# Second attention of a two-layer model: VectorE's small jobs moved between the two maxima of the next half slot

## The chip, the cores and the metric

The kernel runs on one core of a Trainium2 chip. Its engines work side by side, each through its own list of instructions in order: TensorE (PE, matmuls and transposes), VectorE (DVE), ScalarE (ACT), GpSimd (POOL) and SyncE (SP, which here only issues transfers). They wait for each other through semaphores. The metric is the device time of one execution in microseconds (us); the times shown are the median of three runs.

## The reference

Two layers over 8 sequences of 512 tokens with 128 features. Layer 0 is an attention with 16 heads of 64 and a relative position term, and a mixture of 8 experts, two for each token. Layer 1 is a second attention and a mixture of 8 experts with a capacity of 160 tokens. After each of the four comes the residual sum and a layer norm. The change touches only the second attention:

```python
mixed_q = hidden_states @ wq + bq
mixed_k = hidden_states @ wk + bk
mixed_v = hidden_states @ wv + bv
glo = jnp.mean(mixed_q, axis=1, keepdims=True)
c = jnp.tanh(mixed_q @ wfq + bfq + (glo @ wfg + bfg))
...
P = jax.nn.sigmoid(p) * key_len
Z = jax.nn.sigmoid(z) * key_len
G = -(j[None, None, None, :] - P[..., None]) ** 2 * 2.0 / Z[..., None] ** 2
...
scores = jnp.einsum('bhqd,bhkd->bhqk', q, k) / jnp.sqrt(jnp.float32(D))
scores = scores + G
probs = jax.nn.softmax(scores, axis=-1)
ctx = jnp.einsum('bhqk,bhkd->bhqd', probs, v)
```

It has 16 heads of 8. p and z are sums of c over a head with weights.

## The kernel before

The second attention (`gauss_attention_phase`) goes through the 8 batches one after the other: a first one, six middle ones in a hardware loop, a last one, and a tail that drains what is left. A batch has 16 slots, four for each of four groups of heads. A slot has two halves, "middle" and "end"; below, 9M and 9E are the two halves of slot 9.

In each half TensorE computes, in this order: a score tile of 128 queries by 512 keys for one head into bank `a_s0`, a transposed score tile for a later stage into `a_st`, a second score tile for another head into bank `a_s1`, and a second transposed tile (`scores`, L1768 and L1772). Then come eight value matmuls of an earlier unit into `a_pv` (L1804). VectorE reads each score tile and takes the negated row maximum (`maxima`, L1932, into `a_nm`). A score tile of the next half may be written only when the maximum over the same bank is done (`max_done`). ScalarE takes the exponential of the two transposed tiles (L1890). The maxima of a group are transposed (nm0 to nm3, L1829), stored in half precision and put by a transfer into a row of the query operand, so that the transposed scores have them subtracted.

Between these runs a series of small jobs that all use one shared PSUM bank, `a_misc`. Their places are written out by hand in two tables, `MIDDLE` and `END` (L1272 to L1274), one job at most in each half. TensorE fills the bank, then ScalarE, VectorE or both read it; TensorE may fill it for the next job when all earlier readers are done (`misc_out`). The jobs are:

- for the batch ahead: XT (transposed tokens, L1387; ScalarE writes the high part, VectorE subtracts it for the low part, L1484), Q, K and F (three matmuls each, L1396 to L1398, read by ScalarE), GB (a gate bias, VectorE, L1494), PZ (L1420, ScalarE's exponential, then VectorE's three steps for the centres, L1501 to L1503), CF (transposed coefficients, L1428, ScalarE), V (L1407 to L1409, VectorE's copy, L1490)
- for the batch at hand: ctx0 and nm0 to nm3 (ScalarE reads these)
- for the batch behind: ctx1 to ctx3 (a transpose, L1815, then VectorE's reciprocal and product, L1938 and L1940), CT (L1821, ScalarE high, VectorE low), OUT (output projection; VectorE's sum, statistics and their aggregation, L1947, L109, L114), RX (transposed normalised rows, L1836, ScalarE high, VectorE low), RL (router logits, L1843 to L1845, VectorE)
- RC and RD, the routing counts, in the last batch and the tail only

`norm` is the end of the second attention's layer norm: VectorE normalises four tiles (L122), GpSimd makes two copies of the result, SyncE stores rows. It waits for an inverse deviation that GpSimd computes after OUT.

`schedule` (L1671 on) is one function that every engine runs with its own table of steps, so all engines go through the same order. `shared_use` finds the batch for a job and calls the engine's step.

Of the kernel before, what the change touches and what calls it, by code (L numbers as in the profile page):

```python
# [82 lines left out]
class Steps:  # L83
# [12 lines left out]
    def step(self, ins):  # L96
        self.done(ins)
        self.wait()
# [1140 lines left out]
def routing_memory(nc, ctx, m):  # L1239
# [24 lines left out]
G = 4  # L1264
# [3 lines left out]
NM_LOADS = 2 * 16  # L1268
PARTS = 7 * 16
ZERO_PARTS = 8  # L1270
PREP = ["XT", "Q", "K", "GB", "F", "PZ", "CF", "V"]
MIDDLE = {4: "nm0", 8: "nm1", 9: "CT", 10: "OUT", 12: "nm2", 13: "RX", 15: "RD"}  # L1272
END = {0: "ctx1", 1: "XT", 2: "Q", 3: "RC", 4: "ctx2", 5: "K", 6: "GB", 7: "F", 8: "ctx3", 9: "PZ", 11: "CF", 12: "ctx0",
       13: "V", 14: "RL", 15: "nm3"}  # L1274
SLOTS = 4 * G
EXPS_AT = {("last", 1): 0, ("tail", 0): 1, ("tail", 15): 2}
CHOSEN_AT = {("last", 2): 0, ("tail", 1): 1, ("tail", 15): 2}
# [6 lines left out]
def part_of(name):  # L1284
    return name if name in ("RC", "RD") else "ahead" if name in PREP else "behind" if name in BEHIND else "own"

def uses(kind):
    order = [t[at] for at in range(SLOTS) for t in (MIDDLE, END) if at in t]
    return [u for u in order if part_of(u) in PARTS_OF[kind]]

def use(kind, b, name):

    if kind == "prep0":
        return PREP.index(name)
    base = len(PREP)
    if kind != "first":
        base = base + len(uses("first")) + len(uses("middle")) * ((b if kind == "middle" else B - 1) - 1)
    if kind == "tail":
        base = base + len(uses("last"))
    return base + uses(kind).index(name)  # L1300
# [313 lines left out]
def gauss_attention_phase(nc, io, out, m):  # L1614
# [8 lines left out]
    with ExitStack() as ctx:  # L1623
# [13 lines left out]
        ct_h, ct_l = (sb(n, [P, S], F16) for n in ("a_ct_h", "a_ct_l"))  # L1637
# [3 lines left out]
        xr_h, xr_l = (sb(n, [P, S], F16) for n in ("a_xr_h", "a_xr_l"))  # L1641
        res = sb("a_res", [P, QC, D], F32)
        scale = [sb(f"a_scale{k}", [P, QC], F32) for k in range(4)]
        r = m.r
# [16 lines left out]
        ct_hi, pvs_done, ctx_steps, xres_done = names("ct_hi", "pvs_done", "ctx_steps", "xres_done")  # L1661
        s_mm, max_done, exp_done = ([sem(f"a_{n}{k}") for k in range(2)] for n in ("s_mm", "max_done", "exp_done"))
        st_mm = g_.st_mm
        nm_in = [sem(f"a_nm_in{g}") for g in range(G)]
# [3 lines left out]
        def schedule(eng, do):  # L1668

            def step(name, *args):
                if name in do:
                    do[name](*args)

            def shared_use(name, kind, b):
                part = part_of(name)
                if part in PARTS_OF[kind]:
                    batch = {"ahead": b + 1, "behind": b - 1}.get(part, b)
                    if name[-1] in "0123":  # L1680
                        step(name[:-1], kind, b, batch, int(name[-1]))
                    else:
                        step(name, kind, b, batch)

            def batch(kind, b):
                behind, own = kind != "first", kind != "tail"
                for at in range(SLOTS):
                    g, s = divmod(at, G)
                    step("slot", kind, b, at)
                    head = (b, g, s) if own else None  # L1690
                    unit = ((b, (at - 6) // G, (at - 6) % G, kind == "first" and at == 6) if at >= 6 and own
                            else (b - 1, (at + 10) // G, (at + 10) % G, False) if at < 6 and behind else None)
                    for half, table in ((0, MIDDLE), (1, END)):
                        step("scores", half, head, unit)
                        if kind == "tail" and at == 6:
                            step("value", b - 1, G - 1, QC - 1, half)
                        if half and s == 2 and (at < 8 and behind or at >= 8 and own):
                            step("group_end", *((b - 1, g + 2) if at < 8 else (b, g - 2)))
                        if at in table:
                            shared_use(table[at], kind, b)  # L1700
                    if at == 11 and behind:
                        step("norm", b - 1)

            step("setup")
            batch("first", 0)
            with eng.Fori(1, B - 1) as b:
                batch("middle", b)
            batch("last", B - 1)
            batch("tail", B)
# [197 lines left out]
        def _(dve):  # L1907
# [9 lines left out]

            used, low, turns = prep.dve(dve)

            def maxima(half, head, unit):  # L1920
                if not head:
                    return
                b, g, s = head
                n = 16 * b + 4 * g + s
                if s == 0 and half == 0:

                    dve.wait_ge(nm_in[(g + 2) % G], NM_LOADS * (b + 1) if g >= 2 else NM_LOADS * b)
                c = 2 * (s % 2) + half
                for j in range(2):
                    hh = 2 * (s // 2) + j  # L1930
                    dve.wait_ge(s_mm[j], 2 * n + half + 1)
                    nc.vector.tensor_reduce(nm[g % 2][:, c, hh:hh + 1], s_ps[j][:, :], AX.X, ALU.max,  # L1932
                                            negate=True).then_inc(max_done[j], 1)

            def context(kind, b, cb, g):
                used(kind, b, f"ctx{g}")
# [48 lines left out]
            def place(name):  # L1985
                def run(kind, b, _):
                    h = INSTALMENT[kind, name]
                    (c0, n), c1, hs, k = ROUTED[h], sum(ROUTED[h]), slice(ROUTED[h][0], sum(ROUTED[h])), prefix_in[0]
                    used(kind, b, name)
                    nc.vector.tensor_copy(r.counts[h][:, :], misc[:, 0:2 * n * E1]).then_inc(misc_out, 1)  # L1990
                    dve.wait_ge(misc_out, use(kind, b, name) + 1)
                    running = r.counts[h][:, 0:n * E1].rearrange("p (c e) -> p c e", e=E1)
                    totals = r.counts[h][:, n * E1:].rearrange("p (c e) -> p c e", e=E1)
                    if h == 0:
                        routing.done(nc.vector.memset(r.prefix[k][:, 0:1, :], 0.0))
                    else:
                        before = r.counts[h - 1][:, (2 * ROUTED[h - 1][1] - 1) * E1:].unsqueeze(1)
                        routing.done(nc.vector.tensor_tensor(r.prefix[k][:, c0:c0 + 1, :], r.prefix[k][:, c0 - 1:c0, :], before, ALU.add))
                    routing.step(nc.vector.tensor_copy(r.prefix[k][:, c0 + 1:c1, :], totals[:, 0:n - 1, :]))
                    d = 1  # L2000
                    while d < n:
                        old, new = r.prefix[k], r.prefix[1 - k]
                        routing.done(nc.vector.tensor_copy(new[:, c0:c0 + d, :], old[:, c0:c0 + d, :]))
                        routing.step(nc.vector.tensor_tensor(new[:, c0 + d:c1, :], old[:, c0 + d:c1, :], old[:, c0:c1 - d, :], ALU.add))
                        k, d = 1 - k, 2 * d
                    prefix_in[0] = k
                    routing.step(nc.vector.tensor_tensor(r.held[:, hs, :], running, r.prefix[k][:, hs, :], ALU.add))
                    routing.step(nc.vector.tensor_tensor(r.onehot_pos[:, hs, :], r.held[:, hs, :], r.onehot[:, hs, :], ALU.mult))
                    routing.step(nc.vector.tensor_reduce(r.pos[:, hs], r.onehot_pos[:, hs, :], AX.X, ALU.add))

                    routing.done(nc.vector.scalar_tensor_tensor(r.slot[:, hs], r.best[:, hs], float(CAP), r.pos[:, hs], ALU.mult, ALU.add))
                    routing.done(nc.vector.tensor_scalar(r.over[:, hs], r.pos[:, hs], float(CAP), None, ALU.is_gt))
                    routing.step(nc.vector.tensor_scalar(r.away[:, hs], r.best[:, hs], float(NT), OUT_OF_RANGE, ALU.mult, ALU.add))
                    routing.step(nc.vector.tensor_tensor(r.over[:, hs], r.over[:, hs], r.away[:, hs], ALU.mult))
                    routing.step(nc.vector.scalar_tensor_tensor(r.slot[:, hs], r.slot[:, hs], -1.0, r.over[:, hs], ALU.add, ALU.add))
                    nc.vector.tensor_copy(r.to_slot[:, hs], r.slot[:, hs]).then_inc(r.slots_done, 1)
                return run

            def slot(kind, b, at):
# [6 lines left out]
                if (kind, at) in CHOSEN_AT:  # L2026
                    choose(CHOSEN_AT[kind, at])

            schedule(dve, {"slot": slot, "RX": low("RX", xr_h, xr_l, r.rx_hi), "RL": logits, "RC": place("RC"), "RD": place("RD"), **turns, "scores": maxima, "ctx": context, "CT": low("CT", ct_h, ct_l, ct_hi), "OUT": output, "norm": norm})

        @block.gpsimd
        def _(pool):
# [343 lines left out]
```

## Time and profile before

| | |
|---|---|
| median of three runs | 1611.47 us (1609.98 to 1611.98) |
| profiled execution | 1612.34 us |
| its span, first to last instruction | 1610.6 us |
| busy: PE | 1448.2 us, 90% |
| busy: DVE | 1116.6 us, 69% |
| busy: ACT | 956.0 us, 59% |
| busy: POOL | 755.3 us, 47% |
| second attention, first to last score | 1046.2 to 1519.0 us |
| mean granted TensorE clock | 0.962 |

The profile is one execution. Each engine's busy time is the sum of its instructions; a PE that is busy is not one at its peak, since two matmuls on different rows of the array run at once and both are counted. The rows that matter here are single instructions in order of time, because the change moves work by less than a microsecond many times over. The granted clock is 1.00 where TensorE runs at its full 2.4 GHz and 0.5 where it runs at 1.2 GHz.

### The profile page before, as it was taken

The numbers are of one execution on the slowest core, as the hardware profiler recorded it, in microseconds if no ns is written. First come the engines' busy times: TensorE is split into PE (matmuls) and PEld (weight loads), VectorE is DVE, ScalarE is ACT, GpSimd is POOL, SyncE is SP. The second block draws the span as 40 slices with busy tenths as digits, with TensorE's granted clock in tenths as the row PEclk, the third lists the DMA queues.
The fourth block names the chain that finished last, engine by engine and source line by source line (L and its number), as shares of the span: only waits on it lengthen the run. The fifth ranks groups of instructions, "written<-read, shape, count | busy, mean of one in ns | idle before, by whom it ended". The sixth has DMA issues, their size and how long they took to land. (4 is left out here: it accounts for less than half of the span.)

```text
span 1610.6 us, 37407 instructions
## 1 busy us (share of the span) xinstructions
PE 1448.2 (90%) x12185; PEld 808.4 (50%) x12185; DVE 1116.6 (69%) x2581; ACT 956.0 (59%) x2056; POOL 755.3 (47%) x944
## 2 busy tenths in 40 slices
PE   5999999999999999999978998878888888887837
PEld 3666666666666666666655666522333332332225
DVE  5567666666757657666677777778888888888732
ACT  2555555555555555555556887737667677675721
POOL 4656656655665665665564444511222231232633
PEclk9999999999999999999989999959999999999968
DMA  6101000000100000000000000150111111111000
GB/s 193 26 21 28 22 20 23 23 20 20 26 20 20 26 20 20 22 25 20 20 17 2 0 0 1 37 156 24 51 33 36 43 33 49 36 36 34 18 24 17
DMA packets 71099, 50.82 MB, mean 32 GB/s; under 512 B 30875, under 2 KB 59408, under 8 KB 70896
## 3 DMA queue, kind: packets, MB, share of 16 engines
q1 hardware_dynamic: 67936, 45.70, 10.3%
q10 hardware_dynamic: 1760, 3.02, 0.6%
q0 software_dynamic: 1344, 1.33, 0.3%
q8 instruction: 35, 0.57, 0.2%
q14 instruction: 24, 0.20, 0.1%
HBM read 38.18 MB, written 13.28 MB: 32 GB/s over the span
## 5 line engine op out<-in xcount | busy, mean ns | idle before, releaser
L608 ACT ACTIVATE prob<-score_ps,nmax 128x512 f32<-128x512 f32 (+3 forms) x512 | 266.8, 528 | 181.7 <-DVE nmax L669 181.7
L669 DVE TENSOR_REDUCE nmax<-score_ps 128x1 f32<-128x512 f32 (+3 forms) x512 | 225.0, 481 | 200.2 <-PE score_ps L488 195.4
L1932 DVE TENSOR_REDUCE a_nm<-a_s 128x1 f16<-128x512 f32 x512 | 324.0, 685 | 46.1 <-PE a_s L1768 43.6
L1890 ACT ACTIVATE a_pt<-a_st 128x1024 f32<-128x1024 f32 x256 | 261.7, 1024 | 122.1 <-PE a_st L1772 121.3
L1768 PE MATMUL a_s<-a_kop,a_qop 64*128 64x512 f16 x512 | 185.0, 405 | 62.6 <-DVE a_nm L1932 54.6
L786 POOL TENSOR_SCALAR_AFFINE_SELECT k_h<-k 64x512 f16<-64x512 f32 x130 | 79.1, 609 | 266.7 <-ACT k L635 256.4
L500 PE MATMUL pt_ps<-ident,prob 128*128 128x128 f32 x1280 | 186.2, 276 | 2.4 <-ACT pt L617 1.4
L617 ACT ACTIVATE pt<-pt_ps 128x512 f32<-128x512 f32 (+1 forms) x192 | 102.9, 536 | 139.4 <-PE pt_ps L500 139.4
L1772 PE MATMUL a_st<-a_qop,a_kop 64*128 64x512 f16 x512 | 175.1, 395 | 0.0
L1804 PE MATMUL a_pv<-a_pt,a_vaug 128*32 128x256 f32 x2048 | 167.4, 399 | 8.0 <-ACT a_pvs L1895 6.1
L789 POOL TENSOR_TENSOR k_l<-k,k_h 64x512 f16<-64x512 f32 x130 | 152.6, 1174 | 10.8
L500 PEld LDWEIGHTS pt_ps<-ident,prob 128*128 128x128 f32 x1280 | 140.6, 141 | 33.7 <-issue 11.6
L789 POOL TENSOR_TENSOR q_l<-q,q_h 128x512 f16<-128x512 f32 x130 | 151.1, 1162 | 10.8
L485 PE MATMUL score_ps<-k_h,q_h 128*128 128x512 f16 (+3 forms) x512 | 153.6, 300 | 0.6 <-POOL q_l L789 0.6
L486 PE MATMUL score_ps<-k_l,q_h 128*128 128x512 f16 (+3 forms) x512 | 153.6, 300 | 0.0
L487 PE MATMUL score_ps<-k_h,q_l 128*128 128x512 f16 (+3 forms) x512 | 153.4, 300 | 0.0
L512 PE MATMUL pv_ps<-pt,v 128*64 128x512 f32 (+3 forms) x1024 | 151.9, 439 | 0.0
L684 DVE COPY pt<-pt_ps 128x512 f32<-128x512 f32 (+1 forms) x192 | 114.7, 597 | 49.6 <-PE pt_ps L500 47.2
L1768 PEld LDWEIGHTS a_s<-a_kop,a_qop 64*128 64x128 f16 x512 | 41.7, 94 | 184.6 <-DVE a_nm L1932 144.9
L512 PEld LDWEIGHTS pv_ps<-pt,v 128*64 128x64 f32 x1024 | 67.9, 136 | 115.8 <-issue 106.2
L689 DVE SCALAR_TENSOR_TENSOR q<-proj_ps,q_bias,q_mult 128x512 f32<-128x512 f32 x130 | 97.3, 748 | 28.2 <-PE proj_ps L456 27.9
L1210 POOL TENSOR_TENSOR hid_l<-hid,hid_h 128x512 f16<-128x512 f32 x65 | 75.3, 1162 | 78.9 <-ACT hid_h L1115 78.7
(376 smaller groups left out, 3038.6 us busy)
## 6 DMA issues: line engine op xcount, KB each, us to landing
r_bc<-r_parts SPq DMA_DIRECT2D x128, 128.0 KB, 2.8
a_qop<-q_parts SPq DMA_DIRECT2D x64, 64.0 KB, 1.9
a_kop<-k_parts SPq DMA_DIRECT2D x64, 64.0 KB, 1.9
x_tok<-in_L_attn_input_dram SPq DMA_DIRECT2D x4, 512.0 KB, 12.4
r_parts<-rsum SPq DMA_DIRECT2D x128, 2.0 KB, 2.1
q_parts<-a_q_h SPq DMA_DIRECT2D x16, 128.0 KB, 2.3
k_parts<-a_k_h SPq DMA_DIRECT2D x16, 128.0 KB, 2.3
e_w<-in_L_ffn_w_dram SPq DMA_DIRECT2D x1, 2048.0 KB, 10.5
```

Source lines behind the costliest of these rows:

```text
L485: nc.tensor.matmul(o, q_h[h][:, qs], m.k_h[h][:, 0:w], start=True, stop=False)
L486: nc.tensor.matmul(o, q_h[h][:, qs], m.k_l[h][:, 0:w], start=False, stop=False)
L500: mm = nc.tensor.transpose(pt_ps[use % 2][:, col + (c - j) * P:col + (c - j + 1) * P], prob[h][:, P_OFF[c] + j * P:P_OFF[c] + (j + 1) * P] ...
L512: mm = nc.tensor.matmul(pv_ps[64 * h:64 * h + 64, j * P:S], v32[k][:, j, 64 * h:64 * h + 64], pt[h][k][:, J_OFF[j]:J_OFF[j] + S - j * P], ...
L608: ins = nc.scalar.activation(prob[h][:, P_OFF[c]:P_OFF[c] + w], score_ps[u][:, col:col + w], ACT.Exp, bias=nmax[h][:, c:c + 1], accum_out= ...
L669: ins = nc.vector.tensor_reduce(nmax[h][:, c:c + 1], score_ps[u][:, col:col + P * (c + 1)], AX.X, ALU.max, negate=True)
L789: return nc.gpsimd.tensor_tensor(lo, src, hi, ALU.subtract)
L1768: nc.tensor.matmul(s_ps[j][:, :], qop[tile_rows[j], t, g, c * P:(c + 1) * P], kop[tile_rows[j], t, g, :], start=True, stop=True).then_inc( ...
L1772: return nc.tensor.matmul(st_ps[t][:, j, :], kop[tile_rows[j], t, g, kc * P:(kc + 1) * P], qop[tile_rows[j], t, g, :], start=True, stop=True)
L1804: mm = nc.tensor.matmul(pv_ps[32 * hh:32 * hh + 32, cols], vaug[:, kc, G * g + hh, :], pt[kc % 2][hh // 2][:, hh % 2, cols], start=(kc == ...
L1890: nc.scalar.activation(pt[kc % 2][r][:, :, :], st_ps[r][:, :, :], ACT.Exp, scale=1.0 / SC).then_inc(exp_done[r], 1)
L1932: nc.vector.tensor_reduce(nm[g % 2][:, c, hh:hh + 1], s_ps[j][:, :], AX.X, ALU.max, negate=True).then_inc(max_done[j], 1)
```

## The change

VectorE's step `scores` is split into `first_head`, the maximum over `a_s0`, and `second_head`, the maximum over `a_s1`. VectorE no longer does the job of a half behind both maxima of that half. It keeps it, and does it in the next half between the first and the second maximum. This holds in the first, middle and last batches; in the tail, which has no maxima, jobs stay where they are. The other engines have no `second_head` and do a job at its place in the table as before.

The tables change: CT from 9M to 9E, OUT from 10M to 10E, PZ from 9E to 10M, F from 7E to 8E, ctx3 from 8E to 7E, CF from 11E to 12E, ctx0 from 12E to 11E. `norm` moves for all engines from behind 11E to behind 12M.

```diff
-MIDDLE = {4: "nm0", 8: "nm1", 9: "CT", 10: "OUT", 12: "nm2", 13: "RX", 15: "RD"}
-END = {0: "ctx1", 1: "XT", 2: "Q", 3: "RC", 4: "ctx2", 5: "K", 6: "GB", 7: "F", 8: "ctx3", 9: "PZ", 11: "CF", 12: "ctx0",
-       13: "V", 14: "RL", 15: "nm3"}
+MIDDLE = {4: "nm0", 8: "nm1", 10: "PZ", 12: "nm2", 13: "RX", 15: "RD"}
+END = {0: "ctx1", 1: "XT", 2: "Q", 3: "RC", 4: "ctx2", 5: "K", 6: "GB", 7: "ctx3", 8: "F", 9: "CT", 10: "OUT", 11: "ctx0",
+       12: "CF", 13: "V", 14: "RL", 15: "nm3"}
...
+                job = None
                 for at in range(SLOTS):
...
                         step("scores", half, head, unit)
+                        step("first_head", half, head)
...
-                        if at in table:
+                        if "second_head" in do and own:
+                            if job:
+                                shared_use(job, kind, b)
+                            job = table.get(at)
+                            step("second_head", half, head)
+                        elif at in table:
                             shared_use(table[at], kind, b)
-                    if at == 11 and behind:
-                        step("norm", b - 1)
+                        if at == 12 and half == 0 and behind:
+                            step("norm", b - 1)
...
-            def maxima(half, head, unit):
+            def maxima(j):
+                def run(half, head):
...
-                for j in range(2):
-                    hh = 2 * (s // 2) + j
+                    c, hh = 2 * (s % 2) + half, 2 * (s // 2) + j
                     dve.wait_ge(s_mm[j], 2 * n + half + 1)
...
-            schedule(dve, {... "scores": maxima, ...})
+            schedule(dve, {... "first_head": maxima(0), "second_head": maxima(1), ...})
```

## Rows read from the trace of the kernel before

**Rows 1.** Page, costliest groups: busy us, mean ns of one, idle before.
```profile
L1932 DVE TENSOR_REDUCE a_nm<-a_s 128x1 f16<-128x512 f32 x512 | 324.0, 685 | 46.1 <-PE a_s L1768 43.6
```
**Rows 2.** Tile a_s, who waited for it or its bank: us in total, times.
```profile
  PEld a_s L1768: 144.9, 267
```
**Rows 3.** Busy time by stretch, two batches: stretch, length, engines, granted clock, DMA.
```profile
1224.60:1283.50 58.90, 51.38 (x487) 18.25 (x487) 48.61 (x95) 41.42 (x51) 14.39 (x30) 0.97 0.14 38
1342.40:1400.40 58.00, 50.09 (x491) 18.25 (x487) 48.45 (x96) 41.27 (x51) 14.39 (x30) 1.00 0.13 39
```
**Rows 4.** Timeline, TensorE, 0E to 3M: start, us, instruction, idle before and its releaser.
```profile
1344.21 0.66 PE L1815 MATMUL a_misc<-ident,a_pvs 128*128 128x128 f32 x4
1344.79 0.39 PE L1768 MATMUL a_s<-a_kop,a_qop 64*128 64x512 f16 x1
...
1345.33 0.64 PE L1804 MATMUL a_pv<-a_pt,a_vaug 128*32 128x256 f32 x8
1346.14 0.39 PE L1768 MATMUL a_s<-a_kop,a_qop 64*128 64x512 f16 x1 [0.17 <-DVE a_nm L1932]
...
1346.74 0.39 PE L1768 MATMUL a_s<-a_kop,a_qop 64*128 64x512 f16 x1 [0.21 <-DVE a_nm L1932]
...
1347.06 0.64 PE L1804 MATMUL a_pv<-a_pt,a_vaug 128*32 128x256 f32 x8
1347.63 0.66 PE L1387 MATMUL a_misc<-ident,a_xs 128*128 128x128 f32 x4
1348.21 0.39 PE L1768 MATMUL a_s<-a_kop,a_qop 64*128 64x512 f16 x1
...
1351.79 0.39 PE L1396 MATMUL a_misc<-a_xt_h,a_w_h 128*128 128x512 f16 x1
...
1352.54 0.39 PE L1768 MATMUL a_s<-a_kop,a_qop 64*128 64x512 f16 x1
```
**Rows 5.** Timeline, VectorE, the same stretch.
```profile
1344.90 0.26 DVE L1938 RECIPROCAL a_rsum<-a_misc 128x16 f32<-128x16 f32 x1 [0.41 <-PE a_misc L1815]
...
1345.40 2.48 DVE L1932 TENSOR_REDUCE a_nm<-a_s 128x1 f16<-128x512 f32 x4
1348.95 0.69 DVE L1484 TENSOR_TENSOR a_xt_l<-a_misc,a_xt_h 128x512 f16<-128x512 f32 x1 [1.07 <-ACT a_xt_h L1443]
1349.56 2.48 DVE L1932 TENSOR_REDUCE a_nm<-a_s 128x1 f16<-128x512 f32 x4
1352.97 2.49 DVE L1932 TENSOR_REDUCE a_nm<-a_s 128x1 f16<-128x512 f32 x4 [0.93 <-PE a_s L1768]
```
**Rows 6.** Timeline, TensorE, PZ and V, each with the score after it.
```profile
1374.93 1.08 PE L1420 MATMUL a_misc<-a_upz,a_c 128*128 128x32 f32 x8 [0.34 <-DVE a_ct_l L1484]
1375.94 0.39 PE L1768 MATMUL a_s<-a_kop,a_qop 64*128 64x512 f16 x1
...
1391.37 0.23 PE L1407 MATMUL a_misc<-a_w_h,a_xt_h 128*128 128x128 f16 x1 [0.35 <-DVE a_xr_l L1484]
...
1392.15 0.39 PE L1768 MATMUL a_s<-a_kop,a_qop 64*128 64x512 f16 x1
```
**Rows 7.** Timeline, VectorE: CT's low part, OUT's sum, the next maxima.
```profile
1374.18 0.69 DVE L1484 TENSOR_TENSOR a_ct_l<-a_misc,a_ct_h 128x512 f16<-128x512 f32 x1 [0.61 <-ACT a_ct_h L1443]
...
1378.53 0.68 DVE L1947 TENSOR_TENSOR a_y<-a_misc,a_xres 128x512 f32<-128x512 f32 x1
...
1380.45 2.45 DVE L1932 TENSOR_REDUCE a_nm<-a_s 128x1 f16<-128x512 f32 x4
```
**Rows 8.** Timeline, TensorE: first scores of 0M, 5M, 15M and the next 0M.
```profile
1341.55 0.38 PE L1768 MATMUL a_s<-a_kop,a_qop 64*128 64x512 f16 x1 [0.20 <-issue]
...
1358.45 0.39 PE L1768 MATMUL a_s<-a_kop,a_qop 64*128 64x512 f16 x1
...
1395.65 0.39 PE L1768 MATMUL a_s<-a_kop,a_qop 64*128 64x512 f16 x1
...
1399.61 0.38 PE L1768 MATMUL a_s<-a_kop,a_qop 64*128 64x512 f16 x1 [0.23 <-issue]
```

More of the change, by code:

```diff
@@ L1918, in _ @@
             used, low, turns = prep.dve(dve)
-            def maxima(half, head, unit):
[L1921 to L1928, printed above, removed]
-                for j in range(2):
-                    hh = 2 * (s // 2) + j
+            def maxima(j):
+                def run(half, head):
+                    if not head:
+                        return
+                    b, g, s = head
+                    n = 16 * b + 4 * g + s
+                    if s == 0 and half == 0 and j == 0:
+                        dve.wait_ge(nm_in[(g + 2) % G], NM_LOADS * (b + 1) if g >= 2 else NM_LOADS * b)
+                    c, hh = 2 * (s % 2) + half, 2 * (s // 2) + j
                     dve.wait_ge(s_mm[j], 2 * n + half + 1)
@@ L1933, in maxima @@
                                             negate=True).then_inc(max_done[j], 1)
+                return run
             def context(kind, b, cb, g):
@@ L2027, in slot @@
                     choose(CHOSEN_AT[kind, at])
-            schedule(dve, {"slot": slot, "RX": low("RX", xr_h, xr_l, r.rx_hi), "RL": logits, "RC": place("RC"), "RD": place("RD"), **turns, "scores": maxima, "ctx": context, "CT": low("CT", ct_h, ct_l, ct_hi), "OUT": output, "norm": norm})
+            schedule(dve, {"slot": slot, "RX": low("RX", xr_h, xr_l, r.rx_hi), "RL": logits, "RC": place("RC"), "RD": place("RD"), **turns, "first_head": maxima(0), "second_head": maxima(1), "ctx": context, "CT": low("CT", ct_h, ct_l, ct_hi), "OUT": output, "norm": norm})
         @block.gpsimd
```

## The prediction

> **What bounds the kernel now.** I read the page for the size of the stage and then went where the change works. TensorE's score matmul and VectorE's maximum over it, 512 of each, make the second attention; one maximum lasts 685 ns and 324.0 us of VectorE go into them [rows 1]. The waits at the score tile show the coupling: in 267 cases the score's weight load, first thing in a matmul, waited for a maximum, 144.9 us in all [rows 2]. So neither engine is simply full. They hand two score banks to and fro, and what counts is the handover. A middle batch at full clock takes 1399.61 - 1341.55 = 58.06 us [rows 8]; its stretch has a granted clock of 1.00 and holds about 50 us of TensorE and 48 us of VectorE work [rows 3]. Either engine alone would need less than the batch takes. The loss is in the order.
>
> **The rules of the handover**, read from one batch. I write s1 and s2 for the starts of the two scores of a half slot, D1 and D2 for its two maxima, and number half slots by slot and M or E (middle, end). Clock zero is the batch's first score.
> (a) D1 starts 0.42 after s1 when VectorE is idle (1352.54 to 1352.97); a following maximum starts 0.60 later (four take 2.48 us, each 0.68 long) [rows 4, 5].
> (b) A score starts 0.74 after the start of the maximum that frees its bank (1345.40 to 1346.14) [rows 4, 5].
> (c) The value matmuls start 0.32 after an s2 that had to wait (1346.74 to 1347.06), or 0.54 after an s1 with nothing waiting (1344.79 to 1345.33). The job, or the next s1, follows 0.57 later (1347.06 to 1347.63) [rows 4].
> (d) A job holds TensorE for 0.58 (four transposes, 1347.63 to 1348.21), 0.75 (Q, K, F; 1351.79 to 1352.54), 1.01 (PZ) or 0.78 (V, OUT) [rows 4, 6]. For nm, GB, RL and CF, 0.32, 0.32, 0.39 and 0.33 are my estimates from the batch's timeline.
> (e) VectorE can begin a ctx job 0.69 after TensorE begins it (1344.21 to 1344.90) and needs 0.50. The XT job, which waits for ScalarE's copy, can begin 1.32 after (1347.63 to 1348.95) and needs 0.61 [rows 4, 5].
>
> All of TensorE's work stands in one order: s1, a transposed score, s2, another, the values, the job. So the end of a half slot hangs on the later of its two scores, and **s2 hangs on D2 of the half before**. That is the point on which the forecast turns.
>
> **Part 1, the job between the two maxima.** After a job TensorE is late and VectorE has run dry. Before, a ctx job starts 0.11 after s1 and is over at 0.61, in place of the 0.42 at which D1 could start: 0.3 of its 0.50 lies under the score's own latency, and both maxima are late by 0.19 only. After, D1 starts at 0.42, the job at 1.02, D2 at 1.52 in place of 1.02: late by the full 0.50. Each job that is ready at once therefore costs **0.31 more**: ctx four times a batch; GB and RL by their 0.2, where they were covered wholly. V costs 0.60 after against 0.45 before, when it stood behind a late D2. OUT, 1.92 us (1378.53 to 1380.45) [rows 7], is paid in full both times.
> Jobs that wait for ScalarE gain. XT's D1 starts at 1349.56 against s1 at 1348.21, so 1.35 in place of 0.42, late by 0.93 [rows 4, 5]. After, D1 is on time, the job starts at 1.03, and D2 is late by 0.61: **0.31 less**. CT and RX were ready a little later (CT at 1374.18) [rows 7], so 0.38 less each. The centres behind PZ cost 0.96 both ways. Sum of this part per batch: 4 x 0.31 + 0.2 + 0.2 + 0.15 - 0.31 - 2 x 0.38 = +0.7.
>
> **Part 2, the moved jobs and the shared bank.** TensorE may start a job only when the last reader of the bank is done. A reader between the maxima of the next half slot is not done when TensorE gets there. Before, this stall stood twice: PZ behind CT, 0.34, and V behind RX, 0.35 [rows 6]. After, four pairs stand in adjacent half slots: ctx3 at 7E and nm1 at 8M, CT at 9E and PZ at 10M, ctx0 at 11E and nm2 at 12M, RX at 13M and V at 13E. For a ctx pair, TensorE is ready at 0.54 + 0.57 = 1.11 and the reader ends at 1.03 + 0.58, release 0.06: 1.67, a stall of **0.56**. For CT or RX the reader ends at 1.03 + 0.69, release 0.06: 1.77, a stall of **0.66**. Sum: 2.44 against about 0.8 before, +1.6. The moves also undo the neighbourhoods ctx3-CT-PZ-OUT; that is worth nothing by itself, as the order CT, PZ, OUT remains.
>
> **Part 3, the rest of what moves.** Norm goes behind 12M: on VectorE its 1.1 us delays D1 of 12E rather than of 12M, 0.4 either way. On SyncE the nm2 transfer no longer queues behind the output rows, which feeds 14M and had time before. CF and its transfer come a half slot later; the operand loads for the next batch are then issued by about 56.3 and needed at 60.8, so nothing waits. GpSimd's polynomial and rstd chain need about 4.7 us after the centres; norm's turn comes 7 us after. nm0 to nm3 stay. In the last batch RC's long VectorE job too goes between maxima, +0.3.
>
> **The walk.** With the rules, the s1 times after, counted from the batch's start (start before in brackets): 0E 1.23, 1M 3.25, 1E 4.42, 2M 7.01 (6.67), 2E 8.17, 3M 11.03 (10.99), 5M 16.94 (16.90 [rows 8]), 5E 18.11, 6M 20.86 (20.49), 7M 23.83, 7E 25.31, 8M 27.26 (26.89), 8E 29.25 behind the first stall, 9M 31.17, 9E 32.34, 10M 34.42, 10E 37.20 behind the second, 11M 39.09, 11E 40.83, 12M 44.56 (42.63), as s2 of 11E waits out OUT, 12E 46.55, 13M 48.54, 13E 50.62, 14M 53.17, 14E 54.34, 15M 56.82 (54.10 [rows 8]), next batch **60.76** (58.06 [rows 8]). One half in full, 1M to 2M: D1 3.67, ctx 4.28, D2 4.78; s1 of 1E 4.42, s2 5.53, values 5.85, XT 6.42, end 7.01. The bracketed times without a group are my reading of the same timeline. +2.7 a batch; the parts gave +2.3, the rest is what a late s2 adds where OUT and ctx0 follow each other.
>
> **Sum.** Six middle batches: 6 x 2.7 = 16.4. First batch: ctx0 and its stall 0.9, V 0.3, GB 0.2, XT -0.3, so about +1. Last: ctx1 to ctx3, ctx0, RC and OUT at 0.3, RL 0.2, two stalls 1.1, CT and RX -0.7, so +2.4, taken as +2 since a stall lets VectorE catch up. The drain after it has no scores: nothing. Together +19.3. The profiled execution took 1612.34 us (span 1610.6); it would take 1631.6. The median of 1611.47 becomes **1630.8**.
>
> **Rivals.**
> *The clock pays too.* The batch of 1224.60 had a stretch at half clock (0.97 in the mean) and took 58.9, 0.84 more than the one at 1.00 [rows 3]; the low stretch came behind the stall at OUT. After, two longer gaps stand close together at 10M and 11E. Three of the six middle batches have one such stretch now; if each of the six had two, that is nine more, 9 x 0.84 = 7.6: 1638. The Trainium skill, "TensorE: Matmul & The Clock Gate", section "HAM oscillation — how this bites in real kernels", states that idle gaps throttle the engine again and again; this case's trace has it in three middle batches, so the rule makes this rival possible and not certain. 0.10.
> *The stalls are cheap.* If what TensorE loses at the bank is given back by VectorE catching up, only part 1 stays: 0.7 x 8 = 5.6, 1617. For it: VectorE is nearly as loaded. Against: after each stall VectorE has run dry. 0.10.
> *The late s2 is free, the early s1 is not (faster).* If the values did not stand behind s2, a job between the maxima would be hidden and XT, CT and RX would give back 0.31 + 2 x 0.38 = 1.07 a batch with no ctx cost, less a little stall: 7 x 0.9 = 6, 1605. It decides from the point where s2 finds its bank free before TensorE reaches it. The rows say no: at 1346.74 s2 waited 0.21 for its maximum and the values followed in order [rows 4]. The Trainium skill, "PSUM — Partial Sum Buffer", section "Engine vs sequencer instructions", states that matmuls start and complete in program order, which forbids it; with overtaking the sum would be 1605. 0.08.
> *Nothing comes of it.* The starts shift inside slack, 1611. For it: the two kinds of job have opposite signs. 0.06.
>
> **How the numbers follow.** Forecast as walked (1625 to 1636) 0.66. The range runs from the cheap-stall case to the clock case, 1617 to 1638, and leaves out the last two rivals and the far end of the clock case. A measurement of this kernel tells 0.2%, 3 us, from no change. Faster 0.08, within 0.06, slower 0.86.
>
> **What would show it.** The changed trace should have a batch of 60.8, scores waiting for VectorE mostly at s2 (D2) rather than s1, nm1 and nm2 transposes released by a ctx reader, PZ and V by a low-part subtraction, waits of 0.5 to 0.7; VectorE's idle before the XT, CT and RX subtractions near zero, and its idle before D1 of the half after a ctx job up from nothing to 0.4 or more. If s2 after a ctx job starts as early as now, part 1 is wrong; if nm1 and nm2 start without a wait, part 2 is.

## The result and the profile after

The changed kernel took 1630.36 us (median of 4 runs, 1627.27 to 1633.68) beside 1610.72 for the kernel before: a ratio of 1.0121, 95% interval 1.0097 to 1.0144. It is slower by 19.6 us. The forecast was 1630.8, within 1617 to 1638. The profiled execution took 1633.68 us, its span is 1631.9; it is the slowest of the four runs, so the shares below are those of the slowest run.

The page's first part and costliest groups, kernel after. The maxima now stand at L1938, the scores at L1775.

```profile
span 1631.9 us, 37407 instructions
PE 1457.2 (89%) x12185; PEld 807.1 (49%) x12185; DVE 1115.2 (68%) x2581; ACT 956.8 (59%) x2056; POOL 756.0 (46%) x944
...
L1938 DVE TENSOR_REDUCE a_nm<-a_s 128x1 f16<-128x512 f32 x512 | 330.7, 686 | 102.6 <-PE a_s L1775 100.0
```

The instructions are the same in number and length; a maximum took 685 ns before [rows 1]. What grew is idle time: VectorE waited 100.0 us for scores in front of its maxima, 43.6 before [rows 1]. Not all of that is new. VectorE used to wait in front of its jobs too, and over the whole second attention it is idle for 105 us after and 83 before, 22 more. TensorE's waits for maxima at the score tile hardly grew in sum, 203.2 us beside 199.6, but there are 329 of them in place of 389: fewer and longer.

Busy time by stretch, the six middle batches after (stretch, length, engines, granted clock):

```profile
1107.38:1167.86 60.48, 50.31 (x488) 17.82 (x488) 48.27 (x95) 41.69 (x51) 14.40 (x30) 1.00 0.14 39
1167.86:1229.62 61.76, 52.69 (x487) 18.35 (x488) 48.48 (x95) 41.62 (x51) 14.40 (x30) 0.94 0.13 36
1229.62:1290.04 60.42, 50.31 (x487) 17.81 (x488) 48.28 (x95) 41.52 (x51) 14.39 (x30) 1.00 0.13 37
1290.04:1351.70 61.66, 51.79 (x488) 18.22 (x488) 48.34 (x95) 41.56 (x51) 14.40 (x30) 0.97 0.13 36
1351.70:1413.50 61.80, 51.81 (x487) 18.18 (x488) 48.38 (x95) 41.57 (x51) 14.38 (x30) 0.97 0.13 36
1413.50:1475.03 61.53, 52.65 (x487) 18.44 (x488) 48.47 (x95) 41.46 (x50) 14.40 (x30) 0.94 0.13 37
```

Two batches ran at a clock of 1.00 throughout: 60.48 and 60.42, where the kernel before has 58.06 [rows 8]. Four had a stretch at half clock and took 61.5 to 61.8. Before, the first three middle batches had one. Here are the middle batches before, again by stretch:

```profile
1107.28:1165.85 58.57, 51.34 (x489) 18.43 (x488) 48.69 (x95) 41.48 (x51) 14.38 (x30) 0.97 0.14 40
1165.85:1224.60 58.75, 51.48 (x488) 18.33 (x488) 48.69 (x95) 41.44 (x51) 14.38 (x30) 0.97 0.13 38
1224.60:1283.52 58.92, 51.39 (x488) 18.26 (x488) 48.61 (x95) 41.44 (x51) 14.39 (x30) 0.97 0.14 38
1283.52:1341.55 58.03, 50.15 (x488) 18.28 (x488) 48.51 (x95) 41.31 (x51) 14.39 (x30) 1.00 0.13 39
...
1399.61:1457.42 57.81, 50.13 (x487) 18.31 (x488) 48.51 (x95) 41.15 (x50) 14.38 (x30) 1.00 0.14 39
```

So the span's 21.3 us divide as follows. At full clock a batch costs 60.45 against 58.05, 2.4 more, times six 14.4. The half-clock stretches: after, four batches together 4.95 above 60.45; before, three together 2.1 above 58.05; that is 2.9 more. The first batch (61.05 before, 60.88 after) gives 0.2 back, the last (61.16 and 64.70) takes 3.5. With 0.2 more for the last middle batch, which is 0.2 shorter than the others before, this is 20.8, and the rest lies outside these stretches. The clock may have a part in the last batch's 3.5 as well. Its stretch before, then after, each counted to the first score of 15E:

```profile
1457.42:1518.58 61.16, 46.47 (x435) 15.40 (x435) 52.34 (x119) 36.49 (x42) 29.01 (x35) 0.94 0.10 25
...
1475.03:1539.73 64.70, 51.45 (x435) 15.80 (x435) 52.04 (x119) 36.90 (x42) 28.79 (x35) 0.84 0.09 24
```

The granted clock fell there from 0.94 to 0.84, and what that makes of the 3.5 no run tells. The first batch ran more than half of its time at half clock in both kernels, a clock of 0.72 in the mean, so the full-clock prices don't describe it.

The timeline of TensorE after a ctx1 and after an XT job (the first scores of 1M and 1E, the second of 1E with the values, then both of 2E), kernel after:

```profile
1232.87 0.39 PE L1775 MATMUL a_s<-a_kop,a_qop 64*128 64x512 f16 x1
...
1234.05 0.39 PE L1775 MATMUL a_s<-a_kop,a_qop 64*128 64x512 f16 x1
...
1235.13 0.39 PE L1775 MATMUL a_s<-a_kop,a_qop 64*128 64x512 f16 x1 [0.70 <-DVE a_nm L1938]
...
1235.45 0.64 PE L1811 MATMUL a_pv<-a_pt,a_vaug 128*32 128x256 f32 x8
...
1237.78 0.39 PE L1775 MATMUL a_s<-a_kop,a_qop 64*128 64x512 f16 x1
...
1238.98 0.39 PE L1775 MATMUL a_s<-a_kop,a_qop 64*128 64x512 f16 x1 [0.81 <-DVE a_nm L1938]
```

VectorE in the same stretch (1M, 1E and the start of 2M):

```profile
1233.30 0.69 DVE L1938 TENSOR_REDUCE a_nm<-a_s 128x1 f16<-128x512 f32 x1 [0.72 <-PE a_s L1775]
1233.90 0.25 DVE L1945 RECIPROCAL a_rsum<-a_misc 128x16 f32<-128x16 f32 x1
1234.18 0.29 DVE L1947 TENSOR_TENSOR a_ctx<-a_misc,a_rsum 128x128 f32<-128x128 f32 x1
1234.39 1.88 DVE L1938 TENSOR_REDUCE a_nm<-a_s 128x1 f16<-128x512 f32 x3
1237.03 0.69 DVE L1938 TENSOR_REDUCE a_nm<-a_s 128x1 f16<-128x512 f32 x1 [0.77 <-PE a_s L1775]
1237.64 0.68 DVE L1484 TENSOR_TENSOR a_xt_l<-a_misc,a_xt_h 128x512 f16<-128x512 f32 x1
```

Read it against [rows 4, 5]. The first score of 1E now starts 1.18 after that of 1M (1.35 before), and then the second waits until 1.08 behind it (0.60 before), with the values behind. The first score gained 0.17 and the second lost 0.48, so the half slot ends 0.3 later. VectorE stood idle for 0.72 before D1, the time in which the ctx job used to run. XT lost its idle 1.07 [rows 5] and starts straight behind the maximum.

The shared bank and OUT, TensorE, kernel after:

```profile
1258.39 0.39 PE L1836 MATMUL a_misc<-a_ident,a_nm 128*4 128x128 f16 x4 [0.48 <-DVE a_ctx L1947]
...
1265.65 1.08 PE L1420 MATMUL a_misc<-a_upz,a_c 128*128 128x32 f32 x8 [0.59 <-DVE a_ct_l L1484]
...
1270.27 0.39 PE L1775 MATMUL a_s<-a_kop,a_qop 64*128 64x512 f16 x1
...
1272.47 0.39 PE L1775 MATMUL a_s<-a_kop,a_qop 64*128 64x512 f16 x1 [1.81 <-DVE a_nm L1938]
```

The waits of the stage by who waited for whom (us in total, times, longest), kernel after:

```profile
PE a_misc L1836 <- DVE a_ctx L1947: 5.7, 12, 0.6
...
PE a_misc L1407 <- DVE a_xr_l L1484: 3.6, 6, 0.6
PE a_misc L1420 <- DVE a_ct_l L1484: 3.6, 6, 0.6
```

The last two rows above are slot 11E: its second score waited 1.81 for the second maximum of 11M, which stands behind OUT. nm1 and nm2 wait for a ctx reader twice a batch, 0.48 each; PZ and V for a low part, 0.60 each, where they waited 0.34 and 0.35 [rows 6]. All four pairs of the forecast are there.

### The profile page after: what moved, and what is told of

The parts are those of the page before. It is cut to its first block and busy times, and to the rows that moved or that the text cites. A ratio compares the mean times of both kernels' runs of the same rounds, so it can differ in the third digit from the quotient of the medians.

```text
span 1631.9 us, 37407 instructions
## 1 busy us (share of the span) xinstructions
PE 1457.2 (89%) x12185; PEld 807.1 (49%) x12185; DVE 1115.2 (68%) x2581; ACT 956.8 (59%) x2056; POOL 756.0 (46%) x944
## 5 line engine op out<-in xcount | busy, mean ns | idle before, releaser
L1938 DVE TENSOR_REDUCE a_nm<-a_s 128x1 f16<-128x512 f32 x512 | 330.7, 686 | 102.6 <-PE a_s L1775 100.0
L1775 PE MATMUL a_s<-a_kop,a_qop 64*128 64x512 f16 x512 | 187.3, 412 | 66.2 <-DVE a_nm L1938 57.7
L1811 PE MATMUL a_pv<-a_pt,a_vaug 128*32 128x256 f32 x2048 | 170.9, 407 | 7.8 <-ACT a_pvs L1902 5.7
L1775 PEld LDWEIGHTS a_s<-a_kop,a_qop 64*128 64x128 f16 x512 | 40.3, 94 | 184.2 <-DVE a_nm L1938 145.5
L488 PE MATMUL score_ps<-causal,ident_bf 128*128 128x128 bf16 x512 | 112.2, 219 | 0.0
## 6 DMA issues: line engine op xcount, KB each, us to landing
x_tok<-in_L_attn_input_dram SPq DMA_DIRECT2D x4, 512.0 KB, 13.1
```

The source lines that it names most:

```text
L1775: nc.tensor.matmul(s_ps[j][:, :], qop[tile_rows[j], t, g, c * P:(c + 1) * P], kop[tile_rows[j], t, g, :], start=True, stop=True).then_inc( ...
L1811: mm = nc.tensor.matmul(pv_ps[32 * hh:32 * hh + 32, cols], vaug[:, kc, G * g + hh, :], pt[kc % 2][hh // 2][:, hh % 2, cols], start=(kc == ...
```

## The experiments

late_old_tables, tables_alone, ctx12_late and waiting_late ran on a chip on which the kernel before took 1611.0. For tables_old_norm, xt_rx_late, after_nm1_later and out_split it took 1628.4, for the remaining runs 1626.4, each on another chip. Every ratio is to the kernel before beside it on the same chip; there is a trace of the kernel before from the first result alone. In the edits, LATE is the set of jobs that VectorE does between the maxima of the next half; the others it does at once, behind both maxima.

**One part alone: the late job with the old tables (late_old_tables).** MIDDLE, END and norm as in the kernel before, schedule as in the changed one.

```diff
-MIDDLE = {4: "nm0", 8: "nm1", 10: "PZ", 12: "nm2", 13: "RX", 15: "RD"}
+MIDDLE = {4: "nm0", 8: "nm1", 9: "CT", 10: "OUT", 12: "nm2", 13: "RX", 15: "RD"}
...
-                        if at == 12 and half == 0 and behind:
-                            step("norm", b - 1)
+                    if at == 11 and behind:
+                        step("norm", b - 1)
```

> The kernel before with its own tables and its own place of norm; only VectorE's job goes between the two maxima of the next half. The theory (a late second maximum holds the value matmuls, and readers that are late hold the shared bank): prices +0.7 us a batch, four adjacent pairs stall (ctx3-CT, CT-PZ, ctx0-RX, RX-V: 0.56 + 0.66 + 0.56 + 0.66, less the 0.7 of two stalls before), so +2.4 a batch and about +17 in all, 1628. The rival that the moved tables cause the loss: 1611 or less, 1605 if the late job alone gives back what XT, CT and RX can.

Measured 1626.46, ratio 1.0101 (1.0084 to 1.0117). A batch at full clock, by stretch:

```profile
1169.50:1229.63 60.13, 50.07 (x488) 17.98 (x488) 48.46 (x95) 41.32 (x51) 14.39 (x30) 1.00 0.13 37
```

60.13 is 2.1 above the kernel before; 2.4 was expected. The late job alone makes most of the loss. With the jobs late, the moved tables add 0.3 a batch (60.42 and 60.13).

**The other part alone: the new tables, every job at once (tables_alone).**

```diff
+LATE = []
...
                             job = table.get(at)
                             step("second_head", half, head)
+                            if job and job not in LATE:
+                                shared_use(job, kind, b)
+                                job = None
```

> The changed kernel's tables and norm behind 12M, with VectorE's jobs behind both maxima of their own half, as before the change. The theory: no reader is late, ctx3-nm1 and ctx0-nm2 find the bank free (reader over 0.61 after the score, TensorE there at 1.11), CT-PZ and RX-V stall 0.35 as before, norm costs the same 0.4: 1611, within 3. The rival that the tables cause the loss: 1625 or more.

Measured 1618.68, ratio 1.0050 (1.0031 to 1.0069). The expectation missed: the tables cost 7.7 by themselves. The batch stretches:

```profile
1108.34:1167.43 59.09, 50.48 (x489) 18.14 (x488) 48.33 (x95) 41.45 (x51) 14.38 (x30) 1.00 0.14 40
1167.43:1226.76 59.33, 51.72 (x487) 18.60 (x488) 48.48 (x95) 41.45 (x51) 14.38 (x30) 0.97 0.13 38
```

At full clock a batch takes 59.09, 1.04 more than before. Five of the six middle batches had a half-clock stretch, against three. I had taken norm's new place for the cause (tables_old_norm):

> The kernel tables_alone (new tables, VectorE's jobs at once) with norm back behind 11E. Theory: behind 12M norm stood behind ctx0 and pushed the maxima of 12E to 1.48 after the score in place of 0.45, 0.5 or more a batch; back at its place the run is 3 to 5 faster than tables_alone, 1614 to 1616. The rival that the moved OUT, ctx0 and the clock carry all of the 7.7: no change from 1618.7, within 1.5.

The edit is the second half of the first one, norm back behind 11E. Measured: ratio 1.0060 (1.0044 to 1.0077), so the rival holds and norm's place is worth nothing. In the trace its 1.1 us only changes sides, as it delays the first maximum of 12M by 1.2 in place of that of 12E by 1.0. Half of the 1.04 lies between 11E and 13E (7.16 us before, 7.72 in the batch of 59.09), where ctx0 is now at 11E with CF at 12E; the other half was there by 11E, behind OUT (0.47 in this batch, 0.24 in the other five). No run takes the swaps apart, so which of them costs what stays open.

**Price of a job that is ready at once (ctx12_late).**

```diff
+LATE = ['ctx1', 'ctx2']
```

with the old tables and norm.

> The kernel before with two jobs only, ctx1 and ctx2, between the maxima of the next half; no job stands in the half behind them, so no bank stall. The theory: each costs 0.31 more (late by 0.50 in place of 0.19), 14 or so of them in the run: +4.3, 1615; in the trace the second score of 1E and 5E comes 0.3 later from the batch's start than before. The rival that a job in the middle is hidden: the same or up to 2.6 faster, as 14 times 0.19 is given back.

Measured 1616.63, ratio 1.0038 (1.0026 to 1.0049): 5.6 more, with 4.3 expected, which the interval just holds (from 4.2). TensorE, half slots 1M and 1E:

```profile
1110.42 0.39 PE L1779 MATMUL a_s<-a_kop,a_qop 64*128 64x512 f16 x1
...
1111.60 0.39 PE L1779 MATMUL a_s<-a_kop,a_qop 64*128 64x512 f16 x1
...
1112.68 0.39 PE L1779 MATMUL a_s<-a_kop,a_qop 64*128 64x512 f16 x1 [0.70 <-DVE a_nm L1942]
```

This is the picture of the changed kernel, with nothing else altered. From the batch's start, 2M comes at 6.99 (6.67 before) and 6M at 21.13 (20.49): 0.32 for each ctx. The full batch at clock 1.00 took 58.70, 0.65 more. The price of the forecast, 0.31, is shown. Four middle batches had a low stretch where three had one before.

**Late only where VectorE would wait (waiting_late).**

```diff
+LATE = ['CT', 'RX', 'XT']
+MIDDLE = {4: "nm0", 8: "nm1", 9: "CT", 10: "PZ", 12: "nm2", 13: "RX", 14: "V", 15: "RD"}
+END = {0: "ctx1", 1: "XT", 2: "Q", 3: "RC", 4: "ctx2", 5: "K", 6: "GB", 7: "F", 8: "ctx3", 10: "OUT", 11: "CF", 12: "ctx0",
+       14: "RL", 15: "nm3"}
```

> Late are only the three jobs that wait for ScalarE: XT, CT, RX. CT stays at 9M, PZ goes to 10M and OUT to 10E, V goes to 14M, so that nothing stands in the half behind a late reader. The theory: 0.31 + 0.38 + 0.38 less a batch, and up to 0.7 from the two stalls that are gone: -1.1 to -1.8 a batch, 1599 to 1604. The rival that any job between the maxima costs its length (0.6 each, 1.8 a batch): 1615 to 1623.

Measured 1611.05, ratio 0.9992 (0.9980 to 1.0005): nothing. Neither expectation met. XT's gain is in the trace: 3M starts at 10.68 (10.99 before). At 10E, with CT and PZ done in both, the lead is 0.7 (35.80 and 36.53). At 11E, where OUT is paid in both, only 0.1 of it is left (41.00 and 41.11), and 12M comes at 43.07 to 43.69 in the batches with a 3.4 us stretch (42.63 in the full-clock batch before). With OUT a half slot later, TensorE's wait behind it stands in front of 11E, the second score of 11E waits too (0.60 behind the first in place of 0.31), and all six middle batches have a half-clock stretch that starts around there. TensorE and CF run slowly in it:

```profile
1384.16 0.61 PE L1779 MATMUL a_s<-a_kop,a_qop 64*128 64x512 f16 x1 [1.52 <-DVE a_nm L1942]
...
1386.31 0.61 PE L1429 MATMUL a_misc<-a_ident,a_coef 128*128 128x128 f16 x4
```

A score takes 0.61 there in place of 0.39, right behind a gap of 1.52. How much of the lost lead is clock and how much the later OUT, no run tells. So the next version left OUT and CF alone (xt_rx_late), and a later one dealt with OUT itself.

```diff
+LATE = ['RX', 'XT']
-MIDDLE = {... 13: "RX", 15: "RD"}
+MIDDLE = {... 13: "RX", 14: "V", 15: "RD"}
-END = {... 12: "ctx0", 13: "V", 14: "RL", 15: "nm3"}
+END = {... 12: "ctx0", 14: "RL", 15: "nm3"}
```

> The kernel before with XT and RX late, V from 13E to 14M so that nothing stands behind RX's late reader; all else as before. The theory, from the trace of waiting_late: XT gives back 0.31 a batch, RX with the moved V 0.26, with nothing touched around OUT and CF: 7 times 0.57 is 4, so 1607 (against 1611). The rival that a gain of this size is eaten at OUT or by the clock: 1611, within 1.5.

Measured 0.9976 (0.9966 to 0.9986), 3.9 us faster where 4 was expected. Three of its middle batches at full clock took 57.47 to 57.49, 0.57 below 58.05. XT alone makes 0.31 of it by 3M, as forecast; RX and the moved V make the rest. A late job pays when VectorE would otherwise wait for ScalarE. That nothing in the half behind may need the bank is argued: no run has RX late with V behind it and all else as before.

**What a bank stall costs on top (after_nm1_later).** The changed kernel with 8M left empty:

```diff
-MIDDLE = {4: "nm0", 8: "nm1", 10: "PZ", ...}
+MIDDLE = {4: "nm0", 9: "F", 10: "PZ", ...}
-END = {... 7: "ctx3", 8: "F", ...}
+END = {... 7: "ctx3", 8: "nm1", ...}
```

> The changed kernel with nm1 at 8E in place of 8M and F at 9M in place of 8E: 8M is empty, so TensorE no longer waits there for ctx3's late reader. The theory (a late second maximum holds TensorE in any case): the stall of 0.6 at 8M is traded for a second score of 8E that waits 1.1, and 8M to 9E takes as long as now (5.08 us) or 0.25 longer; the whole within 3 of the changed kernel, 1630. The rival that each bank stall is paid in full on top: 0.56 less a batch, 4 less in all, 1626.

Measured 1.0119 (1.0103 to 1.0134) against 1.0121 for the changed kernel on one chip and 1.0129 on another. TensorE there, half slots 8M and 8E:

```profile
1256.18 0.39 PE L1775 MATMUL a_s<-a_kop,a_qop 64*128 64x512 f16 x1
...
1257.35 0.39 PE L1775 MATMUL a_s<-a_kop,a_qop 64*128 64x512 f16 x1
...
1258.44 0.39 PE L1775 MATMUL a_s<-a_kop,a_qop 64*128 64x512 f16 x1 [0.70 <-DVE a_nm L1938]
```

nm1 no longer waits, but the second score of 8E does, and 8M to 9E takes 5.22 in place of 5.07. From 10M on this kernel is 0.2 ahead, and its one middle batch at full clock took 60.24, beside 60.48 and 60.42. So of a stall of 0.48 at most 0.2 came back, where the rival asked for 0.56. The late D2 and the bank stall are for the most part the same lost time, paid once.

**OUT in one piece (out_split).** The kernel before with the statistics cut up and norm behind 12M:

```diff
-                layer_norm_stats(nc, dve, m, 2 * B + cb, y, st, mv)
+            def stats_a(cb):
+                for c in range(2):
+                    nc.vector.bn_stats(st[:, c, :], y[:, c, :])
+            def stats_b(cb):
+                ...
+                        if (at, half) == (10, 1) and behind:
+                            step("stats_a", b - 1)
+                        if (at, half) == (11, 1) and behind:
+                            step("stats_b", b - 1)
```

> The kernel before with the statistics behind OUT cut up: the sum stays at 10M, two of the four bn_stats go behind 10E, the other two and the aggregation behind 11E, norm behind 12M. It tells what the 1.9 us of VectorE in one piece cost. The theory that the long piece drains TensorE and brings the half-clock stretch in slot 11: that stretch is gone from most batches, the gap of 1.5 before the score of 11M is gone, 0.5 to 1.3 less a batch: 1602 to 1607. The rival that VectorE's sum of work is what counts: 1611, within 2, and the low stretches stay.

Measured 0.9974 (0.9960 to 0.9989). Two of its middle batches:

```profile
1107.74:1165.47 57.73, 50.46 (x489) 18.27 (x488) 48.43 (x95) 41.38 (x51) 14.54 (x30) 1.00 0.14 40
1165.47:1223.19 57.72, 50.47 (x487) 18.27 (x488) 48.44 (x95) 41.26 (x51) 14.54 (x30) 1.00 0.14 39
```

All six ran at 1.00 and took 57.5 to 57.73. In the middle batches the low stretch goes with the long piece. The cut is worth something without the clock too: 57.72 is 0.33 below a batch of the kernel before at 1.00.

The same cut in the changed kernel, with stats_a behind 11M (after_split), beside the changed kernel itself (after_again):

> The changed kernel with OUT's statistics cut up: the sum between the maxima of 11M, two bn_stats behind 11M, the rest behind 11E. The theory that part of the change's loss is the clock, brought by 1.9 us of VectorE between two maxima: no half-clock stretch in the middle batches, 59.5 to 60.0 a batch at every batch, ratio 1.006 to 1.008. The rival that the loss is late second maxima and bank stalls alone, without the clock: 1.010 or more.

> The changed kernel itself, for a comparison on this chip with after_split: ratio 1.012.

Measured 1.0041 (1.0027 to 1.0055) and 1.0129 (1.0106 to 1.0151). With the cut every middle batch took 59.3 to 59.6 at a clock of 1.00:

```profile
1106.40:1165.98 59.58, 50.31 (x489) 17.89 (x488) 48.18 (x95) 41.68 (x51) 14.57 (x30) 1.00 0.14 39
```

That is 1.86 more than the kernel before with the cut (57.72). So with the clock out of play the change still costs 1.9 a batch. The batches are as expected, but the ratio of 1.0041 is below the expected 1.006 to 1.008. The drop from 1.0129 is OUT and the clock in the middle batches (61.28 to 59.54 in the mean, 10 us in all) and about 4 outside them, for which no run names the cause.

**A version that beats both.** out_split and xt_rx_late in one (split_xt_rx), and then norm in two halves (split_xt_rx_norm2), two tiles behind 12M and two behind 12E:

```diff
                         if at == 12 and half == 0 and behind:
-                            step("norm", b - 1)
+                            step("norm_a", b - 1)
+                        if at == 12 and half == 1 and behind:
+                            step("norm", b - 1)
```

> out_split and xt_rx_late in one: OUT's statistics cut up, XT and RX late, V at 14M, norm behind 12M. The gains stand at different half slots, so the theory has them add: 0.57 a batch off the 57.72 of out_split, no half-clock stretch in slot 11; ratio to the kernel before 0.995 (8 less). The rival that the second takes back the first: 0.9975.

> split_xt_rx with norm in two halves, two of the four tiles behind 12M and two behind 12E. In out_split norm in one piece put the first maximum of 12E 1.87 after its score. The theory: half of it goes under the time in which VectorE has run dry behind ctx0, 0.3 to 0.5 less a batch than split_xt_rx, ratio 0.993. The rival: VectorE is the bound there and only the sum counts, as split_xt_rx within 0.1%.

Measured 0.9938 (0.9923 to 0.9953) and 0.9923 (0.9909 to 0.9938): 10 and 12.5 us below the kernel before on the same chip by the ratios, 9.2 and 11.4 by the medians. The gains add: 57.15 a batch (57.72 less 0.57), then 56.8:

```profile
1105.94:1162.74 56.80, 50.47 (x488) 18.28 (x488) 48.23 (x95) 41.42 (x51) 14.52 (x30) 1.00 0.15 41
```

## Why the prediction was right, and where it was lucky

**The handover rules and the walk** held half slot by half slot. In the full-clock batch from 1229.62, the walk's start times against the measured: 2M 7.01 and 6.99, 3M 11.03 and 11.00, 5M 16.94 and 16.91, 7M 23.83 and 23.79, 10E 37.20 and 37.04, 11E 40.83 and 40.65, 12M 44.56 and 44.32, next batch 60.76 and 60.42. Its excess of 0.3 comes in half at 7M, where GB makes D2 late by 0.07 and not by the 0.2 I took, and in half from 11E to 13M.

**Part 1**, the price of a late job: right in size and place for a ctx (0.32 by ctx12_late) and for XT (0.31 given back by xt_rx_late). GB cost 0.07 and not 0.2; RX, CT, RL and V were not measured one by one. The old tables with late jobs cost 2.1 a batch.

**Part 2**, the bank: the four pairs and their stalls were there, 0.48 and 0.60 for 0.56 and 0.66. The adding up by parts (+0.7 and +1.6) was wrong in kind: after_nm1_later shows that a stall behind a late ctx mostly stands in for the late D2 and is hardly a cost on top. The walk had this right, the parts did not, and that their +2.3 is near the measured +2.4 is luck. Their sum is also off on its own terms: the two stalls before are 0.34 and 0.35, so 0.7 and not "about 0.8". Of the moved jobs the prediction says that undoing the neighbourhoods "is worth nothing by itself". That step failed: tables_alone costs 1.04 a batch. The two edits make 2.1 and 1.04 alone and 2.4 together; 1.0101 and 1.0050 against 1.0121.

**Part 3**, norm at 0.4 either way: by tables_old_norm its place makes no difference. It delayed a first maximum there by 1.2 or 1.0, not by 0.4.

**The sum** met the median within 0.5 us, and that is partly luck. A batch at full clock came to +2.4, not +2.7 (2 us less over six; 6 x 2.7 is 16.2, not the 16.4 of the sum), and the first batch to -0.2, not +1; the last came to +3.5, not +2, and the half-clock stretches, which I had left to a rival, added 2.9. These errors cancel for the most part: the profiled run, the slowest, grew by 21.3 where 19.3 was forecast, and the four runs spread over 6 us. The clock rival was a real part of the result: four middle batches had its stretch, two of them twice as long, though by far not the 7.6 us it was priced at.

Its condition is a long gap at OUT. Every middle batch has that gap, 1.54 before and 1.81 after, but only three of six and four of six have the stretch. With OUT cut up (out_split, after_split) none has. So the gap is needed here and not enough, and what decides between batches is not shown. The Trainium skill, "TensorE: Matmul & The Clock Gate", section "HAM oscillation — how this bites in real kernels", describes a kernel whose idle gaps throttle the engine again each time. The traces agree only in part: the gaps here are shorter than those that the page names, and of these twelve batches seven had a clock of 0.97 or 0.94 and five stayed at 1.00.

**The faster rival** fell where it was said to decide: s2 waited 0.70 and 0.81 for its maximum, and the values followed 0.32 behind.

## What to carry to other kernels

When two engines hand buffers to and fro, price a moved job by what it does to the second handover of the next round, since an in-order engine stalls all its work there. Time in which an engine waits for its first input is free cover for jobs that are ready; a job between the inputs gives that cover up, so move only those that would themselves make the engine wait. Walk the order through with measured distances; adding the prices of parts can count shared waiting twice. And cut the longest piece that one engine does between two handovers before tuning anything smaller near it.

## What the runs showed of the hardware

Where a low stretch comes in a middle batch, it starts near the gap at OUT. Busy time by stretch, kernel after, the batch from 1290.04, up to slot 11 and then inside it:

```profile
1290.04:1333.00 42.96, 36.30 (x339) 12.64 (x339) 34.44 (x69) 30.04 (x37) 9.41 (x21) 1.00 0.11 31
1333.10:1336.50 3.40, 3.40 (x22) 1.23 (x24) 1.49 (x3) 1.06 (x2) 2.23 (x5) 0.50 0.00 0
```

TensorE ran at 2.4 GHz for 43 us, then stood for 1.81 behind OUT, and 3.4 us at 1.2 GHz followed. Between otherwise equal batches this made 0.5 to 0.9 before the change and 1.1 to 1.4 after it, where two of the four stretches are twice as long. The same gap also stands in batches at 1.00 throughout. In the batch from 1341.55 of the kernel before it is:

```profile
1381.17 0.39 PE L1768 MATMUL a_s<-a_kop,a_qop 64*128 64x512 f16 x1 [1.54 <-DVE a_nm L1932]
```

The changed kernel's last batch took very different times on two chips, the middle ones did not. It took 64.70 on the first chip and 77.97 on the one of after_again, while a middle one took 60.42 and 60.45:

```profile
1228.74:1289.19 60.45, 50.31 (x487) 17.82 (x488) 48.28 (x95) 41.58 (x51) 14.39 (x30) 1.00 0.13 37
1474.18:1552.15 77.97, 53.44 (x435) 16.17 (x435) 51.90 (x119) 37.02 (x42) 31.79 (x37) 0.82 0.08 20
```

Nearly all of these 13 us stand at two places: 8E to 10M took 13.1 in place of 4.4, and 15M to 15E 5.6 in place of 1.4. In the first, VectorE stood for 3.9 before a maximum with nothing in the profile that it waited for:

```profile
1516.12 0.69 DVE L1938 TENSOR_REDUCE a_nm<-a_s 128x1 f16<-128x512 f32 x1 [3.86 <-issue]
```

What that batch has and the others don't is GpSimd's scatter of routed rows and VectorE's routing steps. No run tells whether either is the cause, and there is no trace of the kernel before from a chip of this kind. The two ratios of the changed kernel, 1.0121 and 1.0129, agree within their intervals.
